# The max layers of a graph network: where the edge-attribute product is formed and where it is added to the gathered rows

## The chip, the core and the metric

The kernel runs on one core of a Trainium2 chip. The metric is the time of one execution in device microseconds. Three executions of the kernel before took 6829.79, 6830.46 and 6848.0 us, so the median is 6830.46 us. The kernel is one program: four graph layers with a feed-forward layer behind each, over 3125 nodes of 256 values and 50,000 edges that are sorted by their target node. Everything is float32 but a few masks. The change touches one function, `edge_max`, which runs twice in the fourth graph layer.

## The reference, cut to what matters

This is the fourth graph layer. `hv[src]` has 50,000 rows of 256 values, `he` is the edge attribute, 50,000 rows of 64 values.

```
hv = x @ W_in + b_in
for W, b in ((W_u0, b_u0), (W_u1, b_u1)):
    m = jnp.concatenate([hv[src], he], axis=-1)
    m = jax.nn.relu(m @ W + b)
    msg = jax.ops.segment_max(m, dst, num_segments=n)
    hv = jnp.where(has_in, msg + hv, hv)
return jax.nn.relu(hv @ W_ro + b_ro)
```

The product with `W` is split: the 256 upper rows of `W` are applied once per node (`hv @ W[0:256] + b`, stored in DRAM as `tab`), the 64 lower rows once per edge. So for each edge one row of `tab` is fetched, the product of the edge's 64 attributes with `W[256:320]` is added, and the running maximum over the edges of one target node is taken. The relu is the maximum with zero, which the scan starts from.

## The kernel before, in words

`edge_max` works on blocks of 512 edges (`GP`), 98 of them per call (`RG`), 196 in both calls. Names that the code uses: `P` is 128, `D` 256, `KD` 2 (halves of 128 of the 256 values), `Q` 4 (tiles of 128 edges in a block, and also the number of buffers in each ring), `W` 16, `EA` 64. Five engines run their own lists of instructions and meet at semaphores:

- POOL (L2452) gathers the 512 rows of `tab` into `max_rows`, with four indirect DMAs per block. The ring holds four blocks. Before it gathers block n it waits until block n-4 has been added up (semaphore `mixed`).
- SP (L2464, L2468) loads the attributes (`att`, already turned in DRAM: 64 partitions, edges along the free side) and the mask `same`, which is 0 where a new target node begins.
- TensorE, in `edges` (L2483), makes the attribute product: four products of 128 edges by 256 values into the banks `ps_e`, two signals `made` per block. In `turn` (L2493) it transposes the sum `msg` in eight pieces of 128 by 128 into `ps_t`, so that the 256 values stand on the partitions and the 512 edges along the free side; two signals `turned`. In `give_back` (L2504) it transposes the result of the scan back in eight pieces; two signals `returned`.
- VectorE, in `mix` (L2546), adds the gathered rows and `ps_e` into `msg`, two additions of 128x512 per block, and in `scan` (L2558) runs two scans of 128x512 per block, the running maximum, from `ps_t` into `run`.
- ScalarE (L2527) copies `ps_b` to `back` and writes 512 rows to DRAM (L2529).

The order on each engine is written out by hand. On TensorE one turn of the loop is `turn(n+1)`, `edges(n+2)`, `give_back(n)`; on VectorE `scan(n)`, `mix(n+2)`. TensorE's `turn(n)` waits for both additions of block n, its `edges(n)` for the additions of block n-1, since `ps_e` has one pair of banks; each addition waits for its `made`. PSUM's eight banks are used up: two for `ps_e`, four for `ps_t` (two blocks), two for `ps_b`.

Of the kernel before, what the change touches and what calls it, by code (L numbers as in the profile page):

```python
# [6 lines left out]
ALU = mybir.AluOpType  # L7
ACT = mybir.ActivationFunctionType
F32 = mybir.dt.float32
# [7 lines left out]
P = 128  # L17
# [2405 lines left out]
def edge_max(nc, g, table, w_dram):  # L2423


    with Phase(nc) as ph:
        sb, ps, sem = ph.sb, ph.ps, ph.sem
        rows = sb("max_rows", [P, W, D], F32)
        w = sb("w", [EA, D], F32)
        att = sb("att", [EA, W, P], F32)  # L2430
        same = sb("same", [P, Q, GP], BF16)
        msg = sb("msg", [P, W, D], F32)
        run = sb("run", [P, Q, KD, GP], F32)
        back = sb("back", [P, W, D], F32)
        ps_e = ps("ps_e", [P, 2, 512])
        ps_t = ps("ps_t", [P, 2, KD, 512])
        ps_b = ps("ps_b", [P, 2, 512])
# [3 lines left out]
        stored = [sem(f"stored{b}") for b in range(Q)]  # L2441
        w_in, zeroed, made, mixed, turned, ran, returned, taken = (sem(x) for x in (
            "w_in", "zeroed", "made", "mixed", "turned", "ran", "returned", "taken"))
        with nc.Block() as block:
            @block.gpsimd
            def _(pool):
                for n in range(RG):
                    b = n % Q
                    if n >= Q:
                        pool.wait_ge(mixed, 2 * (n - Q) + 2)  # L2450
                    for j in range(Q):
                        nc.gpsimd.indirect_dma_start(  # L2452
                            out=rows[:, b * Q + j, :], out_offset=None, in_=table,
                            in_offset=bass.IndirectOffsetOnAxis(ap=g.src_r[:, n * Q + j:n * Q + j + 1], axis=0)
                        ).then_inc(got[b], 16)

            @block.sync
            def _(sp):
                sp.dma_start(w[:], w_dram).then_inc(w_in, 16)
                for n in range(RG):  # L2460
                    b = n % Q
                    if n >= Q:
                        sp.wait_ge(made, 2 * (n - Q) + 2)
                    sp.dma_start(att[:, b * Q:(b + 1) * Q, :], g.ins["attr_t"][n * Q:(n + 1) * Q, :, :].rearrange("r e l -> e r l")  # L2464
                                 ).then_inc(att_in[b], 16)
                    if n >= Q:
                        sp.wait_ge(ran, 2 * (n - Q) + 2)
                    sp.dma_start(same[:, b, :], g.same_rows[n * GP:(n + 1) * GP].partition_broadcast(P)).then_inc(same_in[b], 16)  # L2468
# [3 lines left out]
            def _(pe):  # L2472
# [3 lines left out]
                def edges(n):  # L2476
                    b = n % Q
                    pe.wait_ge(att_in[b], 16 * (n // Q) + 16)
                    for k in range(2):
                        if n:  # L2480
                            pe.wait_ge(mixed, 2 * (n - 1) + k + 1)
                        for j in range(2):
                            ins = t.matmul(ps_e[:, k, j * D:(j + 1) * D], att[:, b * Q + 2 * k + j, :], w[:], start=True, stop=True)  # L2483
                        ins.then_inc(made, 1)

                def turn(n):
                    b = n % Q
                    if n >= 2:
                        pe.wait_ge(ran, 2 * (n - 2) + 2)
                    pe.wait_ge(mixed, 2 * n + 2)  # L2490
                    for c in range(KD):
                        for j in range(Q):
                            ins = t.transpose(ps_t[:, n % 2, c, j * P:(j + 1) * P], msg[:, b * Q + j, c * P:(c + 1) * P], g.ident[:])  # L2493
                        ins.then_inc(turned, 1)

                def give_back(n):
                    b = n % Q
                    pe.wait_ge(ran, 2 * n + 2)
                    for k in range(2):
# [35 lines left out]
            def _(dve):  # L2535
                v = nc.vector

                def mix(n):
                    b = n % Q
                    dve.wait_ge(got[b], 64 * (n // Q) + 64)  # L2540
                    if n >= Q:
                        dve.wait_ge(turned, KD * (n - Q) + KD)
                    for k in range(2):
                        dve.wait_ge(made, 2 * n + k + 1)
                        s = b * Q + 2 * k
                        v.tensor_tensor(msg[:, s:s + 2, :], rows[:, s:s + 2, :],  # L2546
                                        ps_e[:, k, :].rearrange("p (j d) -> p j d", j=2), ALU.add).then_inc(mixed, 1)

                def scan(n):
# [4 lines left out]
                    for c in range(KD):  # L2554
                        dve.wait_ge(turned, KD * n + c + 1)
                        if n:
                            dve.wait_ge(ran, KD * (n - 1) + c + 1)
                        v.tensor_tensor_scan(run[:, b, c, :], same[:, b, :], ps_t[:, n % 2, c, :], run[:, (b - 1) % Q, c, GP - 1:GP],  # L2558
                                             ALU.mult, ALU.max).then_inc(ran, 1)

                v.memset(run[:, Q - 1, :, :], 0.0).then_inc(zeroed, 1)
                dve.wait_ge(zeroed, 1)
                mix(0)
                mix(1)
                for n in range(RG):
                    scan(n)
                    if n + 2 < RG:
                        mix(n + 2)

# [503 lines left out]
```

## Time and profile before

| what | value |
|---|---|
| median of three executions | 6830.46 us |
| span of the profiled execution | 6822.1 us |
| first call of `edge_max` | about 5143 to 5795 us of the span |
| second call | about 5859 to 6511 us |
| TensorE busy in the span | 4796.2 us (70%) |
| VectorE busy | 3317.7 us (49%) |
| POOL busy | 3256.3 us (48%) |

The execution that was profiled took 6822.1 us from its first instruction to its last; the median of the timed ones is 8.4 us, 0.12%, above that. Times in the rows are microseconds from the start of the span. `PE` is TensorE's matmul side and `PEld` its weight loads, `DVE` is VectorE, `ACT` ScalarE, `SPq` and `ACTq` the issuing of DMAs. `PEclk` or the granted clock is the share of TensorE's full clock: 1.00 is 2.4 GHz, 0.50 is 1.2 GHz. What stands in brackets behind a row is how long the engine was idle before it and what ended that. A float32 matmul shows as two instructions in the trace, a transpose as one, so one block has eight `edges` instructions, eight of `turn` and eight of `give_back`. The names behind "DMA" in such brackets can be another transfer's that uses the same semaphore.

### The profile page before, as it was taken

To read this page: it belongs to the slowest core of one execution; us is meant where nothing else is said; L and a number is where in the kernel's file an instruction comes from. 1 tells how busy PE (TensorE), PEld (TensorE's weight loads), DVE (VectorE), ACT (ScalarE), POOL (GpSimd) and SP (SyncE) were. 2 spreads that over 40 slices of the span, in tenths; PEclk is the share of its full clock that TensorE was granted. 3 is DMA by queue.
4 is the path that set the end of the run, shared out by engine and by line. 5 is a ranking of instruction groups with operands and counts; after the bars stand their busy time and mean duration, and the time that the engine had idled before them with its cause. 6 is when DMAs were issued, how large, how long until landed. Compare 5 with 4: busy or idle time off the path is not lost. (4 is left out here: it accounts for less than half of the span.)

```text
span 6822.1 us, 83340 instructions
## 1 busy us (share of the span) xinstructions
PE 4796.2 (70%) x21859; PEld 3705.9 (54%) x21860; DVE 3317.7 (49%) x8140; ACT 1583.2 (23%) x4023; POOL 3256.3 (48%) x2940
## 2 busy tenths in 40 slices
PE   3666576999844438699959566466567877688868
PEld 2666455677433326477759434244445666566645
DVE  5544467323433337622331466588434555355554
ACT  1000075333100008300014222265221111111121
POOL 2666677777566648300020444564325555555510
PEclk8555588999866769899969655598677777777778
DMA  4888655000288856376646344486436776577710
GB/s 131 271 265 272 189 191 168 8 1 1 62 279 283 276 191 235 120 250 219 195 158 211 113 139 138 148 311 232 138 119 176 203 200 196 158 202 202 204 61 24
DMA packets 751400, 1183.52 MB, mean 173 GB/s; under 512 B 100921, under 2 KB 528682, under 8 KB 750982
## 3 DMA queue, kind: packets, MB, share of 16 engines
q1 hardware_dynamic: 366758, 553.94, 26.0%
q0 software_dynamic: 135904, 356.79, 18.8%
q10 hardware_dynamic: 248448, 269.39, 11.7%
q8 instruction: 125, 2.05, 0.1%
q14 instruction: 165, 1.35, 0.1%
HBM read 818.22 MB, written 361.10 MB: 173 GB/s over the span
## 5 line engine op out<-in xcount | busy, mean ns | idle before, releaser
L2452 POOL DMA_INDIRECT max_rows<-tab,src_r x784 | 743.0, 948 | 607.1 <-DVE msg L2546 292.0
L403 POOL DMA_INDIRECT counts<-put_n,put_at x400 | 565.6, 1414 | 212.6 <-issue 134.8
L1009 POOL DMA_INDIRECT late_rows<-tab,src_a x416 | 418.4, 1006 | 317.7 <-DMA slot_rows<-late_rows 177.5
L2546 DVE TENSOR_TENSOR msg<-max_rows,ps_e 128x512 f32<-128x512 f32 x392 | 265.8, 687 | 557.3 <-PE ps_e L2483 158.2
L986 PE MATMUL ps_b<-q,sel_t 128*128 x832 | 277.8, 499 | 367.1 <-DVE sel_t L905 251.4
L707 POOL DMA_INDIRECT logit_rows<-tab,src_a x416 | 416.9, 1002 | 247.9 <-DVE logits L927 136.0
L707 POOL DMA_INDIRECT logit_rows<-tab_kv,src_a x416 | 396.8, 954 | 284.7 <-issue 125.1
L2483 PE MATMUL ps_e<-w,att 64*128 64x256 f32 x1568 | 515.1, 482 | 24.6 <-DMA att<-in_attr_t 17.2
L2558 DVE TENSOR_TENSOR_SCAN run<-same,run,ps_t 128x512 f32<-128x512 bf16 x392 | 479.4, 1265 | 9.8 <-remote 5.5
L2527 ACT ACTIVATE back<-ps_b 128x512 f32<-128x512 f32 x392 | 222.4, 596 | 1094.4 <-PE ps_b L2504 463.3
L826 PE MATMUL ps_a<-msg,sel 128*128 128x264 f32 (+1 forms) x1664 | 412.8, 397 | 90.2 <-DVEq L758 46.7
L2493 PE MATMUL ps_t<-ident,msg 128*128 128x128 f32 x1568 | 299.2, 355 | 232.1 <-DVE msg L2546 227.1
L1520 PE MATMUL ps_a<-side,blocks 128*128 128x512 f32 x1950 | 460.3, 392 | 0.8 <-PE ps_a L1520 0.6
L1937 POOL DMA_INDIRECT slot_rows<-xn,into x100 | 101.9, 1019 | 745.0 <-DVE into L1929 716.1
L986 PEld LDWEIGHTS ps_b<-q,sel_t 128*128 128x128 f32 x832 | 203.7, 254 | 441.7 <-issue 404.0
L2483 PEld LDWEIGHTS ps_e<-w,att 64*128 64x128 f32 x1568 | 354.4, 238 | 135.0 <-issue 73.8
L986 PE MATMUL ps_b<-et,sel_t 128*128 x832 | 246.7, 370 | 252.8 <-DMA att<-in_attr_t 160.6
L826 PEld LDWEIGHTS ps_a<-msg,sel 128*128 128x128 f32 x1664 | 303.7, 191 | 199.0 <-DVE odd L772 58.2
L1520 PEld LDWEIGHTS ps_a<-side,blocks 128*128 128x128 f32 x1950 | 366.1, 188 | 83.0 <-issue 3.1
L638 PE MATMUL ps_o<-w,rows_t 128*128 128x256 f32 (+4 forms) x1000 | 322.9, 455 | 99.2 <-issue 70.0
L2493 PEld LDWEIGHTS ps_t<-ident,msg 128*128 128x128 f32 x1568 | 254.4, 189 | 251.3 <-issue 247.3
L915 DVE CUSTOM_DVE_ANT_0 prod<-logit_rows,ps_b 128x256 f32<-128x256 f32 x416 | 150.2, 417 | 421.9 <-DMA att<-in_attr_t 335.7
(482 smaller groups left out, 9786.7 us busy)
## 6 DMA issues: line engine op xcount, KB each, us to landing
blocks<-counts SPq DMA_DIRECT2D x390, 320.0 KB
slot_rows<-logit_rows ACTq DMA_DIRECT2D x208, 512.0 KB
edge_rows<-slot_rows SPq DMA_DIRECT2D x208, 512.0 KB
seg_rows<-back ACTq DMA_DIRECT2D x196, 512.0 KB
slot_rows<-late_rows SPq DMA_DIRECT2D x104, 512.0 KB
sum_rows<-slot_rows SPq DMA_DIRECT2D x104, 512.0 KB
counts<-zeros ACTq DMA_DIRECT2D x130, 320.0 KB
wf<-in_L_ffn_W SPq DMA_DIRECT2D x57, 512.0 KB
```

The source lines that it names most:

```text
L403: nc.gpsimd.indirect_dma_start(out=g.counts, out_offset=bass.IndirectOffsetOnAxis(ap=g.put_at[:, j:j + 1], axis=0), in_=g.put_n[:, j:j + 1 ...
L638: ins = nc.tensor.matmul(ps_o[:, (n % DEPTH) * NB + b, 0:c1 - c0], turned_rows(n, q), w[:, q // KD, q % KD, c0:c1], start=q == 0, stop=q = ...
L707: self.nc.gpsimd.indirect_dma_start(out=self.rows[:, (n % Q) * Q + j, :], out_offset=None, in_=table, in_offset=bass.IndirectOffsetOnAxis( ...
L826: nc.tensor.matmul(ps_a[:, n % 8, 0:C], sel[:, b % 2, j, :], rhs, start=True, stop=True).then_inc(summed, 1)
L986: ins = nc.tensor.matmul(product(b, j), sel_t[:, b % 2, j, :], node_cols[:, ds(tiles[j], 1), :].rearrange("p a c -> p (a c)"), start=True, ...
L1009: self.nc.gpsimd.indirect_dma_start(out=self.rows[:, b * Q + j, :], out_offset=None, in_=self.g.tab, in_offset=bass.IndirectOffsetOnAxis(a ...
L1520: ins = nc.tensor.matmul(ps_a[:, q % 2, :], blocks[:, k % RC, n % CH, :], both(side[:, n, :, :]), start=n == 0, stop=i == 0 and n == NT - 1)
L2452: nc.gpsimd.indirect_dma_start(out=rows[:, b * Q + j, :], out_offset=None, in_=table, in_offset=bass.IndirectOffsetOnAxis(ap=g.src_r[:, n ...
L2483: ins = t.matmul(ps_e[:, k, j * D:(j + 1) * D], att[:, b * Q + 2 * k + j, :], w[:], start=True, stop=True)
L2493: ins = t.transpose(ps_t[:, n % 2, c, j * P:(j + 1) * P], msg[:, b * Q + j, c * P:(c + 1) * P], g.ident[:])
L2546: v.tensor_tensor(msg[:, s:s + 2, :], rows[:, s:s + 2, :], ps_e[:, k, :].rearrange("p (j d) -> p j d", j=2), ALU.add).then_inc(mixed, 1)
L2558: v.tensor_tensor_scan(run[:, b, c, :], same[:, b, :], ps_t[:, n % 2, c, :], run[:, (b - 1) % Q, c, GP - 1:GP], ALU.mult, ALU.max).then_in ...
```

## The change

VectorE's addition is gone. TensorE forms the attribute product already turned, with the weights as the loaded side and the 512 edges as the moving side, straight into the banks that the scan reads (`start=True, stop=False`). The gathered rows are then transposed onto it, accumulating in PSUM (`start=False`, with `is_transpose`). `ps_e` and `msg` go away; the banks that become free give `ps_t` a third block (`R = 3`). POOL now waits for `turned` of block n-4 in place of `mixed`. `made` is signalled once per block and is waited for by SP alone. `edges(n)` waits for the scan of block n-3, half by half. `turn(n)` waits for the gathered rows themselves. VectorE runs only scans.

```
-        ps_e = ps("ps_e", [P, 2, 512])
-        ps_t = ps("ps_t", [P, 2, KD, 512])
+        ps_t = ps("ps_t", [P, R, KD, 512])
...
                     if n >= Q:
-                        pool.wait_ge(mixed, 2 * (n - Q) + 2)
+                        pool.wait_ge(turned, KD * (n - Q) + KD)
...
-                        sp.wait_ge(made, 2 * (n - Q) + 2)
+                        sp.wait_ge(made, n - Q + 1)
...
-                    for k in range(2):
-                        if n:
-                            pe.wait_ge(mixed, 2 * (n - 1) + k + 1)
-                        for j in range(2):
-                            ins = t.matmul(ps_e[:, k, j * D:(j + 1) * D], att[:, b * Q + 2 * k + j, :], w[:], start=True, stop=True)
-                        ins.then_inc(made, 1)
+                    for c in range(KD):
+                        if n >= R:
+                            pe.wait_ge(ran, KD * (n - R) + c + 1)
+                        ins = t.matmul(ps_t[:, n % R, c, :], w[:, c * P:(c + 1) * P], att[:, b, :], start=True, stop=False)
+                    ins.then_inc(made, 1)
 
                 def turn(n):
                     b = n % Q
-                    if n >= 2:
-                        pe.wait_ge(ran, 2 * (n - 2) + 2)
-                    pe.wait_ge(mixed, 2 * n + 2)
+                    pe.wait_ge(got[b], 64 * (n // Q) + 64)
                     for c in range(KD):
                         for j in range(Q):
-                            ins = t.transpose(ps_t[:, n % 2, c, j * P:(j + 1) * P], msg[:, b * Q + j, c * P:(c + 1) * P], g.ident[:])
+                            ins = t.matmul(ps_t[:, n % R, c, j * P:(j + 1) * P], rows[:, b * Q + j, c * P:(c + 1) * P], g.ident[:],
+                                           start=False, stop=j == Q - 1, is_transpose=True)
                         ins.then_inc(turned, 1)
...
-                def mix(n):
-                    b = n % Q
-                    dve.wait_ge(got[b], 64 * (n // Q) + 64)
-                    if n >= Q:
-                        dve.wait_ge(turned, KD * (n - Q) + KD)
-                    for k in range(2):
-                        dve.wait_ge(made, 2 * n + k + 1)
-                        s = b * Q + 2 * k
-                        v.tensor_tensor(msg[:, s:s + 2, :], rows[:, s:s + 2, :],
-                                        ps_e[:, k, :].rearrange("p (j d) -> p j d", j=2), ALU.add).then_inc(mixed, 1)
...
-                mix(0)
-                mix(1)
                 for n in range(RG):
                     scan(n)
-                    if n + 2 < RG:
-                        mix(n + 2)
```

On TensorE, the start of a call before the change, in the program's order (`ps_e<-w,att` is `edges`, `ps_t<-ident,msg` is `turn`, `ps_b<-ident,run` is `give_back`; the size is what one instruction of the program writes):

```order
L2483 MATMUL ps_e<-w,att 128x256 x8
L2493 MATMUL ps_t<-ident,msg 128x128 x16
L2483 MATMUL ps_e<-w,att 128x256 x4
L2504 MATMUL ps_b<-ident,run 128x128 x8
L2493 MATMUL ps_t<-ident,msg 128x128 x8
```

And the same place after it:

```order
L2481 MATMUL ps_t<-att,w 128x512 x4
L2489 MATMUL ps_t<-ident,max_rows 128x128 x16
L2481 MATMUL ps_t<-att,w 128x512 x2
L2501 MATMUL ps_b<-ident,run 128x128 x8
L2489 MATMUL ps_t<-ident,max_rows 128x128 x8
```

The order of the three steps is kept. A block has two products of 512 columns where it had four of 256, and the transposes read the gathered rows instead of the sum.

On VectorE the same place, as a piece of the difference (`msg<-max_rows,ps_e` is `mix`, the other is `scan`; the rows that alternate to the end of the call are cut):

```order
-L2561 MEMSET run 128x1024
-L2546 TENSOR_TENSOR msg<-max_rows,ps_e 128x512 x4
-L2558 SCALAR_TENSOR_TENSOR run<-same,run,ps_t 128x512 x2
-L2546 TENSOR_TENSOR msg<-max_rows,ps_e 128x512 x2
```

```order
L2547 MEMSET run 128x1024
L2544 SCALAR_TENSOR_TENSOR run<-same,run,ps_t 128x512 x196
```

Behind the change, the second of these, the 196 scans of a call stand in one row, with nothing between them.

## Rows read from the trace of the kernel before

**Rows 1.** Windows, both calls: busy us per engine, granted clock, DMA share, GB/s.

```profile
5143.00:5795.00 652.00, 514.94 (x2352) 407.04 (x2352) 365.41 (x393) 111.15 (x196) 371.48 (x392) 0.75 0.72 197
5859.00:6511.00 652.00, 521.19 (x2352) 412.85 (x2352) 365.55 (x393) 111.24 (x196) 371.51 (x392) 0.74 0.72 197
```

**Rows 2.** Groups by line in the first call: busy us, mean ns, idle before.

```profile
L2452 POOL DMA_INDIRECT max_rows<-tab,src_r x392 | 371.5, 948 | 319.9 <-DVE msg L2546 146.8 <-issue 113.2 <-POOLq L98 59.9
L2558 DVE TENSOR_TENSOR_SCAN run<-same,run,ps_t 128x512 f32<-128x512 bf16 x196 | 239.7, 1265 | 3.9 <-DMA moe_y<-y 3.5 <-issue 0.4
L2546 DVE TENSOR_TENSOR msg<-max_rows,ps_e 128x512 f32<-128x512 f32 x196 | 132.9, 687 | 279.4 <-DMA moe_y<-y 134.3 <-PE ps_e L2483 72.2 <-issue 61.1
```

**Rows 3.** Timeline of TensorE: start, us, engine, line, operation; at 1.2 GHz, then 2.4 GHz.

```profile
5230.24 1.91 PE L2493 MATMUL ps_t<-ident,msg 128*128 128x128 f32 x8
5232.08 3.77 PE L2483 MATMUL ps_e<-w,att 64*128 64x256 f32 x8
5235.79 1.97 PE L2504 MATMUL ps_b<-ident,run 128*128 128x128 f32 x8
5237.55 1.91 PE L2493 MATMUL ps_t<-ident,msg 128*128 128x128 f32 x8
...
5242.75 1.06 PE L2493 MATMUL ps_t<-ident,msg 128*128 128x128 f32 x8
5243.74 1.99 PE L2483 MATMUL ps_e<-w,att 64*128 64x256 f32 x8
5245.67 1.09 PE L2504 MATMUL ps_b<-ident,run 128*128 128x128 f32 x8
5246.61 1.06 PE L2493 MATMUL ps_t<-ident,msg 128*128 128x128 f32 x8
5247.60 1.99 PE L2483 MATMUL ps_e<-w,att 64*128 64x256 f32 x8
5249.52 1.17 PE L2504 MATMUL ps_b<-ident,run 128*128 128x128 f32 x8
```

**Rows 4.** Timeline of the other engines: one addition in rows 3, then just behind them.

```profile
5235.90 0.69 DVE L2546 TENSOR_TENSOR msg<-max_rows,ps_e 128x512 f32<-128x512 f32 x1 [0.92 <-PE ps_e L2483]
...
5251.64 0.95 POOL L2452 DMA_INDIRECT max_rows<-tab,src_r  x1 [0.30 <-issue]
5254.54 1.29 DVE L2546 TENSOR_TENSOR msg<-max_rows,ps_e 128x512 f32<-128x512 f32 x2 [5.72 <-DMA moe_y<-y]
5254.62 1.09 ACT L2527 ACTIVATE back<-ps_b 128x512 f32<-128x512 f32 x2 [4.64 <-DMA head_row<-in_L_gnn_att_dst]
5255.97 1.30 PE L2493 MATMUL ps_t<-ident,msg 128*128 128x128 f32 x5 [5.29 <-DVE msg L2546]
```

**Rows 5.** What TensorE's transposes waited for in both calls: us, times.

```profile
  DVE msg L2546: 227.1, 56
```

**Rows 6.** Windows of 3.4 us around rows 3 and 4, columns as in rows 1.

```profile
5237.40:5240.80 3.40, 3.40 (x14) 2.85 (x13) 1.54 (x2) 0.80 (x2) 2.48 (x4) 0.55 0.56 157
...
5251.00:5254.40 3.40, 0.00 (x0) 0.00 (x0) 0.00 (x0) 0.00 (x0) 1.28 (x2) 0.95 0.92 298
5254.40:5257.80 3.40, 1.83 (x8) 1.57 (x8) 3.26 (x4) 1.09 (x2) 1.40 (x2) 0.50 0.44 154
```

**Rows 7.** Timeline of TensorE in a later stage: float32 products of 512 columns.

```profile
6642.55 1.88 PE L2703 MATMUL ps_l<-wz,xt 128*128 128x512 f32 x4
6644.27 1.88 PE L2708 MATMUL ps_f<-wfx,xt 128*128 128x512 f32 x4
```

**Rows 8.** Windows there, columns as in rows 1.

```profile
6640.00:6660.00 20.00, 20.00 (x84) 11.67 (x83) 13.76 (x27) 6.41 (x12) 0.00 (x0) 1.00 0.00 0
```

**Rows 9.** All gathers of both calls: ns min/median/max, first and last start in us.

```profile
L2452 POOL DMA_INDIRECT max_rows<-tab,src_r x784: 943/949/959, 5143.3 to 6488.7; - x196
```

**Rows 10.** Timeline, start of the first call.

```profile
5147.05 0.95 POOL L2452 DMA_INDIRECT max_rows<-tab,src_r  x1 [0.31 <-issue]
5152.81 1.28 DVE L2546 TENSOR_TENSOR msg<-max_rows,ps_e 128x512 f32<-128x512 f32 x2 [8.98 <-DMA max_rows<-tab,src_r]
```

More of the change, by code:

```diff
@@ L2423, in edge_max @@
 def edge_max(nc, g, table, w_dram):
+    R = 3
     with Phase(nc) as ph:
@@ L2429, in edge_max @@
         w = sb("w", [EA, D], F32)
-        att = sb("att", [EA, W, P], F32)
+        att = sb("att", [EA, Q, GP], F32)
         same = sb("same", [P, Q, GP], BF16)
-        msg = sb("msg", [P, W, D], F32)
         run = sb("run", [P, Q, KD, GP], F32)
         back = sb("back", [P, W, D], F32)
-        ps_e = ps("ps_e", [P, 2, 512])
-        ps_t = ps("ps_t", [P, 2, KD, 512])
+        ps_t = ps("ps_t", [P, R, KD, 512])
         ps_b = ps("ps_b", [P, 2, 512])
@@ L2441, in edge_max @@
         stored = [sem(f"stored{b}") for b in range(Q)]
-        w_in, zeroed, made, mixed, turned, ran, returned, taken = (sem(x) for x in (
-            "w_in", "zeroed", "made", "mixed", "turned", "ran", "returned", "taken"))
+        w_in, zeroed, made, turned, ran, returned, taken = (sem(x) for x in (
+            "w_in", "zeroed", "made", "turned", "ran", "returned", "taken"))
         with nc.Block() as block:
@@ L2462, in _ @@
                     if n >= Q:
-                        sp.wait_ge(made, 2 * (n - Q) + 2)
-                    sp.dma_start(att[:, b * Q:(b + 1) * Q, :], g.ins["attr_t"][n * Q:(n + 1) * Q, :, :].rearrange("r e l -> e r l")
+                        sp.wait_ge(made, n - Q + 1)
+                    sp.dma_start(att[:, b, :].rearrange("e (r l) -> e r l", l=P), g.ins["attr_t"][n * Q:(n + 1) * Q, :, :].rearrange("r e l -> e r l")
                                  ).then_inc(att_in[b], 16)
                     if n >= Q:
-                        sp.wait_ge(ran, 2 * (n - Q) + 2)
+                        sp.wait_ge(ran, KD * (n - Q) + KD)
                     sp.dma_start(same[:, b, :], g.same_rows[n * GP:(n + 1) * GP].partition_broadcast(P)).then_inc(same_in[b], 16)
@@ L2497, in give_back @@
                     b = n % Q
-                    pe.wait_ge(ran, 2 * n + 2)
+                    pe.wait_ge(ran, KD * n + KD)
                     for k in range(2):
@@ L2557, in scan @@
                             dve.wait_ge(ran, KD * (n - 1) + c + 1)
-                        v.tensor_tensor_scan(run[:, b, c, :], same[:, b, :], ps_t[:, n % 2, c, :], run[:, (b - 1) % Q, c, GP - 1:GP],
+                        v.tensor_tensor_scan(run[:, b, c, :], same[:, b, :], ps_t[:, n % R, c, :], run[:, (b - 1) % Q, c, GP - 1:GP],
                                              ALU.mult, ALU.max).then_inc(ran, 1)
```

## The prediction

> **What bounds the kernel now.** I read the windows of the two calls first. Each takes 652 us for 98 blocks, 6.65 us a block and 1304 us in all, and no engine is full: TensorE is busy for 515 and 521 us, VectorE for 365, POOL for 371, and the clock granted to TensorE is 0.75 and 0.74, so it is at 1.2 GHz for half of the time [rows 1]. The groups by line show who waits for whom: POOL for VectorE's additions, these for TensorE and for something named a DMA [rows 2], TensorE's transposes for the additions again [rows 5]. It is a loop of engines, not one of them.
>
> The timeline says what one turn of the loop costs. At 1.2 GHz TensorE goes without a gap and a block takes 5237.55 - 5230.24 = 7.31 us; at 2.4 GHz it takes 5246.61 - 5242.75 = 3.86 us [rows 3]. POOL needs four gathers of 0.95 us with 0.30 us between them, 5.0 us a block [rows 4, 9]. So POOL alone would give 5.0, and 6.65 is a mixture of blocks at 7.31, blocks at 3.86, and stops.
>
> A stop is seen behind the fast blocks. TensorE's records end its products of a block at 5249.59 and its transposes back at 5250.69 [rows 3], yet the addition that needs nothing but these products, rows gathered long before, and an idle VectorE begins at 5254.54, and ScalarE's copy, which waits for transposes back alone, at 5254.62 [rows 4]. Two engines are set free within 0.1 us, 5 and 4 us after the work they waited for. I read this as TensorE's signals arriving late, in a stretch in which POOL issues gathers without a pause; they arrive 2 us after the last of these gathers ended at 5252.59 [rows 4]. At 1.2 GHz the signals are prompt: products that end at 5235.85 [rows 3] set free an addition at 5235.90 [rows 4]. The bracket's "DMA" I take to be the shared semaphore. The transposes then begin at 5255.97, after 5.29 us without work, and the clock falls: it is 0.95 in the window with no matmul and 0.50 in the next [rows 6]. Over both calls TensorE's transposes wait 56 times for the additions, 227.1 us, 4.06 us each [rows 5]. So the loop is: fast blocks, a stop, the clock down, slow blocks, the clock up again.
>
> **The change, part by part.** *The products.* Eight instructions of 256 columns a block become four of 512. At 2.4 GHz the eight take 5245.67 - 5243.74 = 1.93 us from their start to the next step's [rows 3], and four float32 ones of 512 columns take 6644.27 - 6642.55 = 1.72 us [rows 7] in a stretch at clock 1.00 [rows 8]. These load 128 rows where ours load 64; the row has no other difference. That is -0.21 us a block. At 1.2 GHz the eight take 5235.79 - 5232.08 = 3.71 us [rows 3]; twice 1.72 would be 3.44. No row shows 512 columns at 1.2 GHz, so between nothing and -0.27; I take -0.2 at either clock. 196 x 0.2 = 39 us, all on the path, since TensorE paces the blocks at either clock. Bounds 0 and -53.
>
> *The transposes.* Still eight of 128x128 a block, one instruction each. That they add to what stands in PSUM is shown by no row. Lower bound nothing; upper bound, if each were handled as an ordinary float32 product in two instructions, eight times 0.12 us more at 2.4 GHz (a transpose is (5243.74 - 5242.75) / 8 = 0.12 us, [rows 3]), about +1 us a block and 196 us. I take 0: same operation, same operand sizes.
>
> *The additions.* 392 of 0.687 us leave VectorE, twice 132.9, 266 us [rows 2]. Where TensorE runs without a gap that is worth nothing, since VectorE is idle for over 40% of a call [rows 1]. It counts where a stop ends: from the moment the late signal is seen to the first transpose is 5255.97 - 5254.54 = 1.43 us, two additions and a handover [rows 4]. After the change no transpose waits for VectorE or for a signal of TensorE's own, only for gathered rows, and those are there early: the fourth gather of the first block begins at 5147.05 and ends at 5148.00, and the addition starts 4.8 us later [rows 10]. 56 stops x 1.43 = 80 us.
>
> *What the late signals meet now.* `turned` sets the scan free, the scan `give_back`. Between the end of `turn(n)` and `give_back(n)` TensorE has `edges(n+1)`, `give_back(n-1)`, `turn(n+1)`, `edges(n+2)`: at 2.4 GHz 1.72 + 0.94 + 0.99 + 1.72 = 5.4 us [rows 3, 7], and two scans take 2.5 us [rows 2]. So a `turned` that is 2.9 us late costs nothing, where a late `made` cost at once. This could end the stops, or move them to `give_back`. There are also fewer signals, five a block for six, and 20 matmul instructions for 24. Against it stands the next part. I count both as 0 and keep the ends as rivals.
>
> *The moved waits.* POOL is let go by `turned(n-4)`, not by `mixed(n-4)`, so a row buffer is held until its transposes end, about 1 us longer in a stop and up to `give_back` and `turn` longer otherwise: 1.8 us at 2.4 GHz, 3.6 at 1.2 [rows 3]. Queued behind POOL's wait are only its own gathers. A block's gathers take 4.7 us and land within 4.8 [rows 9, 10], 9.5 us, and four fast blocks are 4 x 3.65 = 14.6 us; the ring is still deep enough. `edges(n)` waits for the scan of block n-3, which at 2.4 GHz is two blocks, 7.3 us, behind its `turned`: 0. SP's DMAs, their sizes and their order stay, and so does all that ScalarE and its queue do: 0.
>
> *The clock.* Shorter stops would leave it up more often; I put 0, since each stop left would still be 4.06 - 1.43 = 2.6 us.
>
> Sum: 6822.1 - 39 - 80 = 6703 us of span, and with the 8.4 us by which the median stands above the span, 6712 us. Range of this case alone, with the bounds of the products and half to twice the gain at the stops: 6620 to 6790 us.
>
> **The rivals.** *A, POOL sets the pace.* The stops and with them most of the slow blocks go. A call then is 392 gathers x 1.25 = 490 us and what follows the last gather, 6511 - 6488.7 = 22 us [rows 1, 9]: 512 for 652, 2 x 140 = 280 us less, 6550 us. For it: the slack of 2.9 us, two scans a block that need 2.5 of 5.0 us. Against it: signals came late exactly while POOL issued without a pause, and here it would never pause.
>
> *B, the stops stay as long.* They end when POOL pauses, not when VectorE is done, so taking out the additions only moves the wait to `give_back`. Then only the products count: 6830 - 39 = 6791 us. For it: DVE and ACT are set free together, 2 us after POOL's last gather [rows 4].
>
> *C, slower.* Now one late signal, `turned`, holds the scan and POOL too, and the message buffer that let the additions run ahead is gone. Each burst of late signals then empties the pipe, TensorE stands long enough for the clock to fall, and the blocks run at 1.2 GHz with 7.1 us each. All of them slow: 98 x 7.1 + 22 = 718 us a call, 2 x 66 = 132 us more, 6962 us; nine in ten slow and the rest at POOL's 5.0: 6.89 a block, 6877 us. It decides from the point where four in five blocks are slow (0.8 x 7.1 + 0.2 x 5.0 = 6.7). At present, 0.51 of 652 us over 7.31 is 45 of 98 [rows 1, 3]. A rule speaks for this rival. The trace first: the clock rises near the end of the window 5237.40 to 5240.80, whose mean is 0.55 [rows 6], since the blocks behind it have the short durations, and most of what TensorE did there and just before were sixteen transposes from 5235.79 to 5239.46 [rows 3]. The Trainium skill, TensorE: Matmul & The Clock Gate, Part 4: PE-mode transpose, says that transposes do not count as work for the clock in the way matmuls do, and that it does not rise for them; by that rule a kernel with fewer ordinary matmul instructions would stay low and give C's 6962 us. The trace contradicts it here, so I leave C small.
>
> *D, the accumulating transposes cost more than plain ones.* By the bound above up to +196 us; with half of it and the gains 6810 us.
>
> **How the numbers follow.** Likeliest case 0.47, A 0.20, B 0.14, C 0.13, D 0.06. The range for 8 in 10 goes from A's 6550 less a little, 6540, to 6845, which leaves out C and a small part of A and D. A measurement of this kernel can tell 0.3%, 20 us, from no change. Faster than 6810: the likeliest case, A, nearly all of B, some of D, 0.81. Within 20 us: 0.06. Slower: C and the bad half of D, 0.13.
>
> **What would show it.** In the changed profile: no row of `msg`; 784 instructions of 512 columns where 1568 of 256 stood, 1.7 us a block at 2.4 GHz; transposes as long as before (0.12 us each at 2.4 GHz); the idle time before them near nothing and waits of TensorE before `give_back` in its place; a call of about 590 us and a granted clock of 0.75 to 0.8. A call near 512 us with POOL busy in 73% of it shows A; one of 630 us with 56 stops of 4 us shows B; a clock below 0.6 shows C. I am wrong if the stops were not set by late signals, or if they grow as much as the additions gave.

## The result

The changed kernel takes 6725.02 us (median of 4 runs, 6715.43 to 6727.1), the kernel before 6831.03 us beside it. The ratio is 0.9836, with a 95% interval of 0.9821 to 0.9851: 1.6% faster, a small gain that is clear of the noise. The forecast was 6712 us. The profiled execution spans 6721.4 us where the one of before spans 6822.1, 100.7 us less.

The first view is the windows of the two calls, which answer to [rows 1]; the columns are the same (length; busy us of TensorE, its weight loads, VectorE, ScalarE, POOL; granted clock; DMA share; GB/s):

```profile
5143.00:5743.00 600.00, 450.89 (x1960) 283.03 (x1960) 242.98 (x197) 112.39 (x196) 370.45 (x392) 0.80 0.76 214
5807.00:6412.00 605.00, 454.29 (x1960) 284.34 (x1960) 242.26 (x197) 112.21 (x196) 370.49 (x392) 0.80 0.75 213
```

The windows of the calls are 52 and 47 us shorter, 99 of the 100.7 us. TensorE was busy for 514.94 + 521.19 = 1036.1 us [rows 1] and is now for 905.2: 131 us less. VectorE lost its additions and is busy for 122 and 123 us less. POOL's gathers cost what they cost, 370.5 us a call. The clock is 0.80 where it was 0.75 and 0.74.

The groups by line in both calls come next (count; busy us, mean ns; idle time of the engine just before them and what ended it). Of before these are the four that the comparison needs and that no row ahead of the prediction gives for both calls:

```profile
L2452 POOL DMA_INDIRECT max_rows<-tab,src_r x784 | 743.0, 948 | 607.1 <-DVE msg L2546 292.0 <-issue 226.4 <-POOLq L98 88.8
L2483 PE MATMUL ps_e<-w,att 64*128 64x256 f32 x1568 | 515.1, 482 | 24.6 <-DMA att<-in_attr_t 17.2 <-issue 3.7 <-DVE msg L2546 3.6
L2493 PE MATMUL ps_t<-ident,msg 128*128 128x128 f32 x1568 | 299.2, 355 | 232.1 <-DVE msg L2546 227.1 <-issue 4.9
L2504 PE MATMUL ps_b<-ident,run 128*128 128x128 f32 x1568 | 271.4, 327 | 18.2 <-issue 11.7 <-DVE run L2558 4.9 <-ACT back L2527 1.6
```

And of the changed kernel:

```profile
L2451 POOL DMA_INDIRECT max_rows<-tab,src_r x784 | 740.9, 945 | 510.7 <-issue 213.4 <-POOLq L98 90.1 <-PE ps_t L2489 82.8
L2544 DVE TENSOR_TENSOR_SCAN run<-same,run,ps_t 128x512 f32<-128x512 bf16 x392 | 483.4, 1269 | 710.2 <-PE ps_t L2489 188.6 <-PE ps_b L2501 165.3 <-DMA moe_y<-y 154.8
L2481 PE MATMUL ps_t<-att,w 64*128 64x512 f32 x784 | 445.7, 694 | 17.8 <-DMA att<-in_attr_t 17.8
L2501 PE MATMUL ps_b<-ident,run 128*128 128x128 f32 x1568 | 267.1, 319 | 283.6 <-ACT back L2524 219.5 <-issue 52.9 <-DVE run L2544 10.9
L2489 PE MATMUL ps_t<-ident,max_rows 128*128 128x128 f32 x1568 | 249.0, 312 | 1.9 <-DMA max_rows<-tab,src_r 1.8
```

Three things are to be seen. TensorE no longer waits before its transposes (1.9 us for 232.1) but before it gives back (283.6 us for 18.2). Its idle time as a whole did not fall: 24.6 + 232.1 + 18.2 = 274.9 us before, 303.3 now. And POOL is idle for 96 us less (510.7 for 607.1). So TensorE gained no time from shorter waits; it gained it from instructions that ran at 2.4 GHz instead of 1.2. Of 196 groups of eight transposes (two calls of 98 blocks), 80 had the short duration before (under 1.15 us from the first start to the last end) and 138 have it now.

The timeline of TensorE around one stop (start, us, engine, line, operation; in the bracket the idle time before it) answers to [rows 3]:

```profile
5292.17 1.04 PE L2489 MATMUL ps_t<-ident,max_rows 128*128 128x128 f32 x8
5293.13 1.98 PE L2481 MATMUL ps_t<-att,w 64*128 64x512 f32 x4
5295.05 1.09 PE L2501 MATMUL ps_b<-ident,run 128*128 128x128 f32 x8
5295.97 1.04 PE L2489 MATMUL ps_t<-ident,max_rows 128*128 128x128 f32 x8
...
5308.86 1.09 PE L2501 MATMUL ps_b<-ident,run 128*128 128x128 f32 x8
5309.79 1.04 PE L2489 MATMUL ps_t<-ident,max_rows 128*128 128x128 f32 x8
5310.76 1.98 PE L2481 MATMUL ps_t<-att,w 64*128 64x512 f32 x4
5321.71 1.94 PE L2501 MATMUL ps_b<-ident,run 128*128 128x128 f32 x8 [8.98 <-ACT back L2524]
5323.45 1.92 PE L2489 MATMUL ps_t<-ident,max_rows 128*128 128x128 f32 x8
```

A block at 2.4 GHz takes 5295.97 - 5292.17 = 3.80 us (3.86 in [rows 3]). Then TensorE stands for 8.98 us. What it waits for is seen on the other engines, which answers to [rows 4]:

```profile
5317.70 0.95 POOL L2451 DMA_INDIRECT max_rows<-tab,src_r  x1 [0.30 <-issue]
5320.97 1.26 ACT L2524 ACTIVATE back<-ps_b 128x512 f32<-128x512 f32 x2 [13.28 <-DMA tab<-hw]
5321.86 2.45 DVE L2544 TENSOR_TENSOR_SCAN run<-same,run,ps_t 128x512 f32<-128x512 bf16 x2 [8.38 <-DMA moe_y<-y]
5321.99 0.94 POOL L2451 DMA_INDIRECT max_rows<-tab,src_r  x1 [3.34 <-DMA moe_y<-y]
```

What ScalarE copies at 5320.97 are the transposes of 5308.86, which ended at 5309.95, 11 us earlier. VectorE and POOL, which wait for other signals of TensorE, are set free within 1.1 us of it, all of them 2.3 us or more after POOL's last gather ended at 5318.65. That is the pattern of [rows 4], with another engine at the end of the wait. The windows there (columns as in [rows 1]) show what it does to the clock:

```profile
5312.80:5316.20 3.40, 0.00 (x0) 0.00 (x0) 0.68 (x1) 0.00 (x0) 2.74 (x3) 1.00 0.91 229
5316.20:5319.60 3.40, 0.00 (x0) 0.00 (x0) 0.00 (x0) 0.00 (x0) 1.89 (x2) 0.50 0.54 160
5319.60:5323.00 3.40, 1.29 (x6) 1.32 (x7) 1.14 (x1) 1.30 (x3) 0.94 (x1) 0.50 0.07 25
```

### The profile page after: what moved, and what is told of

Read it like the earlier page. It is cut to its first block and busy times, and to the rows that moved or that the text cites. A ratio compares the mean times of both kernels' runs of the same rounds, so it can differ in the third digit from the quotient of the medians.

```text
span 6721.4 us, 80988 instructions
## 1 busy us (share of the span) xinstructions
PE 4661.4 (69%) x21075; PEld 3448.9 (51%) x21076; DVE 3071.9 (46%) x7748; ACT 1586.1 (24%) x4023; POOL 3241.1 (48%) x2940
## 3 DMA queue, kind: packets, MB, share of 16 engines
q8 instruction: 118, 1.93, 0.1%
## 5 line engine op out<-in xcount | busy, mean ns | idle before, releaser
L2451 POOL DMA_INDIRECT max_rows<-tab,src_r x784 | 740.9, 945 | 510.7 <-issue 213.4
L1009 POOL DMA_INDIRECT late_rows<-tab,src_a x416 | 416.6, 1001 | 323.7 <-DMA slot_rows<-late_rows 178.2
L2501 PE MATMUL ps_b<-ident,run 128*128 128x128 f32 x1568 | 267.1, 319 | 283.6 <-ACT back L2524 219.5
L2524 ACT ACTIVATE back<-ps_b 128x512 f32<-128x512 f32 x392 | 224.6, 596 | 989.7 <-DMA tab<-hw 281.0
L2481 PE MATMUL ps_t<-att,w 64*128 64x512 f32 x784 | 445.7, 694 | 17.8 <-DMA att<-in_attr_t 17.8
L2501 PEld LDWEIGHTS ps_b<-ident,run 128*128 128x128 f32 x1568 | 201.9, 162 | 460.6 <-issue 369.7
L986 PEld LDWEIGHTS ps_b<-et,sel_t 128*128 128x128 f32 x832 | 207.7, 310 | 269.9 <-issue 262.0
```

Of the source, the lines that this page charges most:

```text
L986: ins = nc.tensor.matmul(product(b, j), sel_t[:, b % 2, j, :], node_cols[:, ds(tiles[j], 1), :].rearrange("p a c -> p (a c)"), start=True, ...
L1009: self.nc.gpsimd.indirect_dma_start(out=self.rows[:, b * Q + j, :], out_offset=None, in_=self.g.tab, in_offset=bass.IndirectOffsetOnAxis(a ...
L2451: nc.gpsimd.indirect_dma_start(out=rows[:, b * Q + j, :], out_offset=None, in_=table, in_offset=bass.IndirectOffsetOnAxis(ap=g.src_r[:, n ...
L2481: ins = t.matmul(ps_t[:, n % R, c, :], w[:, c * P:(c + 1) * P], att[:, b, :], start=True, stop=False)
L2501: ins = t.transpose(ps_b[:, k, j * D + c * P:j * D + (c + 1) * P], run[:, b, c, (2 * k + j) * P:(2 * k + j + 1) * P], g.ident[:])
L2524: nc.scalar.activation(back[:, s:s + 2, :].rearrange("p j d -> p (j d)"), ps_b[:, k, :], ACT.Copy).then_inc(taken, 1)
```

## The experiments

Twelve kernels were run. All ratios are to the kernel before on the same chip. The runs were spread over several chips, on which the kernel before took 6783 to 6846 us (6831 beside the changed one), so microseconds of different rows compare to about 1%. "Call" is the first call, from the start of TensorE's first record to the start of its last; "idle" is TensorE's idle time before its three groups of matmuls in both calls together.

| kernel | ratio (95%) | call, us | idle, us |
|---|---|---|---|
| before | 1 | 646.3 | 274.9 |
| changed | 0.9836 (0.9821 to 0.9851) | 592.8 | 303.3 |
| e1 plain loads, POOL silent | 0.922 (0.9189 to 0.925) | 380.4 | 20.3 |
| e2 as e1, POOL gathers narrow rows | 0.9821 (0.9791 to 0.9851) | 588.1 | 259.6 |
| e8 kernel before, POOL silent | 0.9251 (0.923 to 0.9272) | 385.7 | 21.8 |
| e3 products of 256 columns | 0.984 (0.9816 to 0.9865) | 588.1 | 236.7 |
| e4 POOL a block less ahead | 0.9826 (0.9803 to 0.9849) | 582.9 | 216.7 |
| e5 two `ps_t` pairs | 0.9838 (0.9819 to 0.9857) | 588.8 | 271.5 |
| e6 three signals for five | 0.985 (0.9832 to 0.9869) | 595.5 | 285.0 |
| e7 additions, nobody waits | 0.983 (0.9812 to 0.9848) | 585.9 | 273.3 |
| e9 crossing, short work | 0.984 (0.9823 to 0.9856) | 590.0 | 220.8 |
| e12 crossing, additions' work | 0.9844 (0.9828 to 0.986) | 592.4 | 218.6 |
| e10 two `ps_b` pairs | 0.9833 (0.9817 to 0.9849) | 590.5 | 204.9 |
| e11 and `give_back` later | 0.9832 (0.9815 to 0.985) | 591.4 | 215.2 |

### Is it POOL that delays the signals?

**e1**, in the changed kernel, takes the gathers out and loads plain rows with one transfer of SyncE a block:

```diff
-                    for j in range(Q):
-                        nc.gpsimd.indirect_dma_start(out=rows[:, b * Q + j, :], ...).then_inc(got[b], 16)
+                    pass
...
+                        sp.wait_ge(turned, KD * (n - Q) + KD)
+                    first = n % 6 * GP
+                    sp.dma_start(rows[:, b * Q:(b + 1) * Q, :], table[first:first + GP, :].rearrange("(j p) d -> p j d", p=P)).then_inc(got[b], 16)
```

> The changed kernel, but the 512 rows of a block are fetched by one plain load from SP's queue (consecutive rows of the table, so the gather is left out and the output is not the reference's); POOL is silent in both calls, the bytes moved are the same. Theory 1, TensorE's signals are held back while POOL issues gathers: no stops, clock near 1.0, TensorE sets the pace with 3.8 us a block, a call 375 to 420 us for 595, the kernel about 6340 us. Rival, the data traffic holds them back (DMA share 0.76 in a call): the stops stay or get denser, a call 550 us or more, since the traffic per us would rise.

**e2** is e1 with POOL issuing as many gathers as before, of 16 values a row, into a buffer that nothing reads:

```diff
+                            out=narrow[:, b * Q + j, :], out_offset=None, in_=table.rearrange("n (k s) -> (n k) s", s=16),
...
+                        ).then_inc(fetched[b], 16)
```

> As the run with plain loads, and beside them POOL issues the same 392 gathers per call into a small side tile, 16 values a row in place of 256: the same number of rows and the same issuing, a sixteenth of the bytes. (Output not the reference's.) Theory 1, it is POOL's issuing: the stops of 2 to 14 us in front of the transposes back return, a call 570 to 620 us. Rival, the traffic: a call as with plain loads, or POOL's own 490 us.

Measured: 6260.65 us for e1, 6669.01 for e2. The transposes back in e1, then in e2 (groups by line, as above), and the first call of e1 (window):

```profile
L2499 PE MATMUL ps_b<-ident,run 128*128 128x128 f32 x1568 | 213.9, 279 | 2.8 <-DVE run L2542 2.8
```

```profile
L2510 PE MATMUL ps_b<-ident,run 128*128 128x128 f32 x1568 | 273.2, 325 | 242.6 <-ACT back L2533 175.9 <-issue 48.5 <-DVE run L2553 17.7
```

```profile
5108.70:5489.10 380.40, 378.78 (x1960) 237.59 (x1960) 240.06 (x196) 105.39 (x195) 0.00 (x0) 0.98 1.05 336
```

With POOL silent there is no stop, the clock is 0.98, and a block takes 3.88 us. With POOL issuing gathers that TensorE does not wait for, a sixteenth as wide, the stops and the 588 us are back. It is the gathers, then, and neither their bytes nor the wait for the rows. POOL's issuing and the many small transfers that each gather starts (one for each row) were not taken apart; "POOL's issuing" below means both.

**e8** is the same edit as e1 in the kernel before, with SyncE's load waiting for `mixed`.

> The kernel before, with the gather of both calls left out: SyncE loads plain rows of the table, one transfer a block, and POOL is silent. The changed kernel with the same edit took 6261 us, 0.922 of the kernel before. Theory 1: the change's gain is that fewer signals cross between engines while POOL holds them up; with POOL silent the two kernels are the same within 15 us: 6250 to 6280 us, no stops, clock about 0.8. Theory 2: the additions cost time by themselves (VectorE's hop of 1.4 us in each block): 6320 to 6370 us, with TensorE idle ahead of its transposes as in the kernel before.

Measured: 6279.3 us. VectorE's two groups:

```profile
L2556 DVE TENSOR_TENSOR_SCAN run<-same,run,ps_t 128x512 f32<-128x512 bf16 x392 | 479.1, 1264 | 0.9 <-PE ps_t L2491 0.9
L2544 DVE TENSOR_TENSOR msg<-max_rows,ps_e 128x512 f32<-128x512 f32 x392 | 269.0, 687 | 42.3 <-PE ps_e L2481 13.2 <-DMA max_rows<-tab 4.5 <-issue 2.4
```

With POOL silent the two kernels are 18.6 us apart, on two chips, two runs each (0.9251 and 0.922, intervals that overlap), with the gathers 106. That is a little more than the 15 us of theory 1, and the time is inside its range: most of the gain exists only while POOL issues. The few microseconds left would be VectorE, which here is busy for 366 of 386 us a call and is idle for 0.9 us before its scans; the changed kernel's is busy for 240.

### Which part of the change gives the gain?

Each of the next runs puts one part back into the changed kernel. **e3**, the products in pieces of 256 columns:

```diff
-                        ins = t.matmul(ps_t[:, n % R, c, :], w[:, c * P:(c + 1) * P], att[:, b, :], start=True, stop=False)
+                        for h in range(2):
+                            ins = t.matmul(ps_t[:, n % R, c, h * D:(h + 1) * D], w[:, c * P:(c + 1) * P], att[:, b, h * D:(h + 1) * D], start=h == 0, stop=False)
```

> The changed kernel with each product of 512 columns cut into two of 256, so 4 products (8 instructions) a block as before the change, nothing else. By the prediction's term for the products it costs 0.2 us a block, 39 us: about 6764 us. If the clock went up in the changed kernel because fewer matmul instructions mean fewer held signals, more: up to 6790. If TensorE's shape costs nothing: 6725.

**e5**, the third pair of banks away: `R = 3` becomes `R = 2`.

> The changed kernel with two pairs of ps_t banks in place of three, so that the products of a block wait for the scan of two blocks before. Theory 1: TensorE's semaphore signals arrive late while POOL issues gathers, and it was the additions on VectorE, with their two hops in each block (made to the addition, mixed to the transposes), that made TensorE stop often and fall to the low clock; the third bank is beside the point, since the scan of block n-2 is long done. Then the ratio to the kernel before stays 0.980 to 0.988, and stops stay ahead of give_back (about 280 us). Theory 2: the gain is the third bank, which takes the scan's slowness off the path. Then the ratio is 0.995 to 1.005, and the products stop for ran.

**e7**, VectorE's additions back in number and size, behind each scan, on a buffer of their own:

```diff
+                        for k in range(2):
...
+                            v.tensor_tensor(spare[:, k, :, :], spare[:, k, :, :], spare[:, k, :, :], ALU.add).then_inc(cleared, 1)
```

> The changed kernel with two additions of 128x512 in each block put back on VectorE behind the scan, as in the kernel before, but on a buffer of their own in SBUF: nothing but VectorE's order waits for them. Theory 1: what cost time was that TensorE waited for the additions, not the time that they took on VectorE: ratio to the kernel before 0.980 to 0.988. Theory 2: what cost time was that the scan began later behind the additions: ratio 0.990 to 1.003, and scan's rows show more time between turned and its start.

**e9**, the crossing to VectorE back, with hardly any work in it:

```diff
-                    pe.wait_ge(got[b], 64 * (n // Q) + 64)
+                    pe.wait_ge(mixed, 2 * n + 2)
...
+                    dve.wait_ge(got[b], 64 * (n // Q) + 64)
+                    dve.wait_ge(made, n + 1)
+                    for k in range(2):
...
+                        v.memset(spare[:, k, :], 0.0).then_inc(mixed, 1)
```

> The changed kernel with the crossing to VectorE put back without its work: VectorE waits for the gather and for made as the additions did, at their place behind the scan, does two memsets of 128x16, each with a signal, and TensorE's transposes wait for these and no more for the gather itself. The memsets feed nothing. Theory 1: the chain TensorE to VectorE to TensorE in each block is what cost time, since made and turned reach VectorE late while POOL issues: TensorE stops ahead of its transposes again, and the ratio to the kernel before is 0.993 to 1.003. Theory 2: it needs the additions' own 1.3 us in that chain; with short ones most of the gain stays: 0.982 to 0.990.

**e12**, the same with the additions' work:

```diff
-                        v.memset(spare[:, k, :], 0.0).then_inc(mixed, 1)
+                        v.tensor_tensor(spare[:, k, :, :], rows[:, s:s + 2, :], rows[:, s:s + 2, :], ALU.add).then_inc(mixed, 1)
```

> As e9, but what VectorE does between the gather and the transposes is as long as the additions of the kernel before: two additions of 128x512 a block (of the gathered rows, into a buffer that nothing reads), for which the transposes wait. Left as in the changed kernel: three ps_t banks, POOL's wait on turned, products that wait only for the scan. The crossing with short work cost nothing (0.984), and the additions with nobody waiting cost nothing (0.983). Theory 1: the change gained because a stop no longer has the additions at its end, about 1.4 us between the late signal and the first transpose, and because the shorter stops leave the clock up for longer: here the stops are back as they were, ratio 0.995 to 1.005, and clock near 0.75. Theory 2: the gain came from what is left as in the changed kernel, above all POOL's wait, which lets it issue in fewer, longer stretches: ratio 0.980 to 0.988, clock near 0.775.

Measured: 0.984, 0.9838, 0.983, 0.984 and 0.9844. Every interval holds the changed kernel's 0.9836, and none reaches 0.99. None of these parts is the gain by itself: not the shape of the products, not the third bank, not VectorE's time, not the crossing, and not the crossing with all its work. In e12 the wait did go back to its old place, which is why this run counts most against my reasons (TensorE's transposes, both calls):

```profile
L2490 PE MATMUL ps_t<-ident,max_rows 128*128 128x128 f32 x1568 | 271.1, 329 | 173.5 <-DVE spare L2556 115.9 <-issue 57.6
```

The stops stand before the transposes again, 51 of over 1 us, but they are 2.5 us long (128.2 us in all) where those of before were 3.9 (59, 232.0 us).

### Do the stops go away with slack or with fewer signals?

**e4** lets POOL run three blocks ahead, not four:

```diff
-                    if n >= Q:
-                        pool.wait_ge(turned, KD * (n - Q) + KD)
+                    if n >= 3:
+                        pool.wait_ge(turned, KD * (n - 3) + KD)
```

> The changed kernel, but POOL waits for the transposes of block n-3 in place of n-4, so its unbroken runs of gathers end a block earlier. Theory 1 (a stop lasts until POOL pauses): stops become shorter, the long ones of 8 to 9 us go to about 4, and there are more of them; the kernel within 6700 to 6740 us. Rival, the depth of the ring is what hides the gathers' way from issue to landing (9.5 us): slower, a call over 620 us, the kernel over 6770.

**e6** signals `turned` and `returned` once a block:

```diff
-                        ins.then_inc(turned, 1)
+                    ins.then_inc(turned, 1)
...
-                        ins.then_inc(returned, 1)
+                    ins.then_inc(returned, 1)
```

> The changed kernel with turned and returned signalled once in a block (3 signals of TensorE in a block for 5); the scan and ACT start up to half a group of transposes (0.5 us at the full clock) later. Theory 1: while POOL issues, TensorE's signals are delivered one by one, 0.7 to 2.1 us apart, so 5 in a block of 3.8 us are more than get through, and 3 are not: the stops ahead of give_back shrink from about 280 us in the two calls to under 150, and the ratio to the kernel before falls to 0.960 to 0.975. Theory 2: signals wait for POOL's pauses whatever their number, so fewer do not help: ratio 0.980 to 0.988, or up to 0.995 from the later starts.

**e10** has two pairs of `ps_b` and two of `ps_t`; **e11** also issues each `give_back` a block later:

```diff
-                        if n:
-                            pe.wait_ge(taken, 2 * (n - 1) + k + 1)
+                        if n >= 2:
+                            pe.wait_ge(taken, 2 * (n - 2) + k + 1)
...
-                    give_back(n)
+                    if n:
+                        give_back(n - 1)
```

> The changed kernel with two pairs of ps_t banks (worth nothing by themselves: 0.9838 for 0.9836) and two pairs of ps_b banks, so that give_back waits for ACT's copies of two blocks before, not one. Theory 1: the stops ahead of give_back are late returned signals, of 2 to 9 us; one block more of slack (3.8 us) takes the short ones and shortens the long: give_back's idle time falls from about 280 to 100 to 160 us, ratio 0.965 to 0.978. Theory 2: POOL holds all of TensorE's signals until it pauses, and it pauses only when TensorE's turned reaches it, so more slack only moves the stop to the next wait (the products' on ran, the transposes' on the gather): ratio 0.980 to 0.988, same idle time in another row.

> As e10, and each give_back one block later in TensorE's order, so that its wait for the scan has a block more too. Theory 1 (slack helps): TensorE's idle time falls below e10's, ratio 0.955 to 0.975. Theory 2 (the stop moves): the idle time stands ahead of the products (ran) and of the transposes (gather), ratio 0.980 to 0.990.

Measured: 0.9826, 0.985, 0.9833 and 0.9832. Fewer signals do not help (e6 stands for 285 us), so theory 1 of e6 is refuted. e4 has the shorter stops that its theory 1 asked for (58 of over 1 us before the two groups of transposes, 3.0 us each, where the changed kernel has 54 of 4.8). A shorter ring and more slack do lower the idle time, to 217, 205 and 215 us from 303, but not the time of a call. In e10 the wait has moved to the products and the transposes, as theory 2 said, but it is a third shorter, which theory 2 did not say:

```profile
L2481 PE MATMUL ps_t<-att,w 64*128 64x512 f32 x784 | 506.8, 771 | 117.8 <-DVE run L2544 69.7 <-issue 30.0 <-DMA att<-in_attr_t 17.8
L2489 PE MATMUL ps_t<-ident,max_rows 128*128 128x128 f32 x1568 | 282.6, 322 | 84.3 <-issue 82.9 <-DMA max_rows<-tab,src_r 1.1
L2501 PE MATMUL ps_b<-ident,run 128*128 128x128 f32 x1568 | 271.6, 328 | 2.8 <-DVE run L2544 2.8
```

and what the stops lost, the clock took: products of 771 ns in the mean for 694, and 92 groups of transposes at the short duration for 138. That is seen throughout the table: eleven kernels (the changed one, e2 to e7, e9 to e12), POOL issuing in each, idle times from 205 to 303 us, and first calls from 583 to 596. No version beats the changed kernel by more than the measurement can tell.

## Why the prediction held, and where it did not

The time (6725 us measured, 6712 forecast) and most of what was to show it came out: no row of `msg`, 784 products, idle time before the transposes near nothing with waits before `give_back` in its place, calls of 593 and 598 us in TensorE's records (about 590 was said), a clock of 0.80. But one of the two signs of being wrong that the prediction names came out too: the stops grew although the additions were gone, from 3.9 us in the mean before the transposes to 4.9 before `give_back`, and TensorE's idle time rose where it should have fallen by 80 us. That the time was right is luck: the two terms that made up the sum, 39 and 80 us, were each worth nothing that the runs could tell, and the gain came through the clock, which stood in it at 0. By its steps:

*The products, -39 us: mis-sized, by all of it.* The four of 512 columns take 5295.05 - 5293.13 = 1.92 us from their start to the next step's; the eight of 256 took 1.93 [rows 3]. At 1.2 GHz the four take 3.71 us (5385.10 to 5388.81 in the changed kernel), as the eight did [rows 3]. The 1.72 us of [rows 7], which the prediction took for ours because "the row has no other difference" than the loaded rows, does not carry over, and the single records show why. Inside a group the instructions of 512 columns begin 0.43 us apart, whether they load 64 rows (changed kernel) or 128 ([rows 7]): the product itself costs the same. The 0.2 us lie at the two ends of our group: its first step takes 0.53 us and its last 0.52, and at both ends the weight load of the group that follows begins only 2 or 3 ns before the instruction that uses it. In the stretch of [rows 7] each load begins 2 ns behind the start of the product before, also where transposes follow, and no time is lost. So cutting the products differently could gain nothing: both cuts have the same two ends. What is special about these ends is that 64 loaded rows meet 128; no run varies that alone. e3 agrees with the whole term (0.984 for 0.9836), though it is weak evidence, since its idle time differs too (237 us). The lower bound of nothing was the value.

```profile
5385.10 3.78 PE L2481 MATMUL ps_t<-att,w 64*128 64x512 f32 x4
5388.81 1.97 PE L2501 MATMUL ps_b<-ident,run 128*128 128x128 f32 x8
```

*The transposes, 0: right.* Eight of them with accumulation take 1.04 us where plain ones took 1.06 [rows 3]. With that rival D is gone.

*The additions, -80 us: the step that failed.* It was "56 stops x 1.43 = 80 us", time from the late signal to the first transpose. TensorE's idle time rose by 28 us. And e12 put two additions of that length back between the signal and the transposes and lost nothing (0.9844). In this kernel a microsecond taken out of a stop is not a microsecond of the call, for the stops and the clock trade with each other.

*The late signals, 0:* the slack of 2.9 us did not end the stops. They moved to `give_back`, 53 of over 1 us with 4.9 us in the mean; that "could move them to `give_back`" was the right half of the sentence.

*The clock, 0: wrong, and it is where TensorE's gain is entered.* TensorE is busy for 131 us less, in fewer blocks at 1.2 GHz, and idle for 28 us more; with rounding at the edges of the windows that is the 99 us of both calls. The products gave nothing and a group of transposes 0.02 us, so all but a few of the 131 us are the clock's.

*The moved waits, 0: this is what the experiments leave.* I charged POOL's wait, from `mixed` to `turned`, as a loss that the ring would hide. That POOL was idle for 96 us less says nothing by itself, for the idle time of every engine with unchanged work shrinks with the call; ScalarE's did by 105 (1094.4 to 989.7). What did change is how POOL issues. In the first call's records POOL issued its 392 gathers in 76 stretches before (59 of them of four gathers, a pause at nearly each block) and in 42 now (mostly 8 or 12 gathers; a pause of over 0.6 us parts two stretches). All variants of the changed kernel with the gathers on have 53 or fewer. But this is as much effect as cause, and e7 with 27 stretches and gathers of 1043 ns takes as long as the changed kernel with 42.

So what is shown: the gain needs POOL's issuing (1.6% with it, 0.3% without, e1 against e8), and it is none of five parts of the change put back alone. What stays open: POOL's wait for `mixed`, the message buffer that makes this wait possible, and the sixth signal of a block (`made` twice) were never put back; a combination may be needed too. The products' wait for the additions was not put back either, but it can be struck from the list: `edges(n+2)` stands right behind `turn(n+1)`, which has waited for the same additions already, and only 3.6 us of the idle time before the products are put down to it in the rows of before. The kernel before with POOL waiting for `turned` would be the next run; it was not tried. Open too is what holds a call at 583 to 596 us in all of these kernels.

The rivals: *A*, POOL paces, needed the stops to go; POOL is busy in 62% of a call, and its own 1.25 us a gather give 490 of 593 us. *B* had the mechanism of the stops right, they only move to `give_back` and do not get shorter, but the products it counted on are worth nothing; by its price the time would be 6830. That the gain came all the same, through the clock, was in no case of mine. *C*, slower with the clock down, is refuted: 0.80 for 0.75. (Its two figures do not go together: the 6962 us include the 22 us behind the last gather, the 6877 do not; with them it would be about 6921.) The kernel now has 1960 TensorE instructions a call for 2352 and as many transposes as before, and the clock is higher. The rule of the Trainium skill, TensorE: Matmul & The Clock Gate, Part 4: PE-mode transpose, that the clock does not engage for transposes, would have let it fall. The trace contradicts it: in the changed kernel TensorE does nothing but sixteen transposes behind a stop, and the clock goes up within the second eight of them (windows from 5286.0 to 5288.9 us and on, columns as in [rows 1]):

```profile
5286.09 1.94 PE L2501 MATMUL ps_b<-ident,run 128*128 128x128 f32 x8 [8.98 <-ACT back L2524]
5287.82 1.57 PE L2489 MATMUL ps_t<-ident,max_rows 128*128 128x128 f32 x8
5289.33 1.98 PE L2481 MATMUL ps_t<-att,w 64*128 64x512 f32 x4
...
5286.00:5288.90 2.90, 2.81 (x14) 2.84 (x15) 2.45 (x2) 1.79 (x3) 1.90 (x3) 0.50 0.46 129
5288.90:5292.00 3.10, 3.10 (x15) 1.69 (x15) 2.45 (x2) 0.01 (x1) 2.49 (x3) 1.00 0.91 243
```

## What to carry to other kernels

When an engine's stops are followed by a lower clock, do not price a stop by its length: e10 took 98 us of idle time out of the changed kernel and gained nothing. Before pricing any edit in such a loop, silence the suspected disturber once (e1); it showed that 6% lay in POOL's issuing and not in the work that was being moved. And a duration for a group of products is taken from rows with the same kind of work before and behind it, for part of it lies at its ends.

## What the runs showed of the hardware

TensorE's signals reach other engines late while POOL issues indirect gathers without a pause and TensorE is at 2.4 GHz. It can be counted on ScalarE, which waits for transposes back alone, at those of its 392 copies before which it stood idle. In the changed kernel, where POOL had gathered for over 60% of the 2.5 us before, 55 of 108 copies at 2.4 GHz began over 1 us behind the end of the transposes, the latest 18.5 us, and 1 of 40 at 1.2 GHz; the other 39 began about 0.1 us behind it or sooner. In e1, with POOL silent and TensorE at 2.4 GHz, all 196 did. The slow clock is no guard against it, though: in e3 27 of 63 such copies at 1.2 GHz were over 1 us late. In the changed kernel's semaphore records of the stop above, `turned`, `made` and `returned` counts rose at 5307.07, 5308.51, 5312.18, 5316.43 and 5320.89 us, one at a time, and then four times within 0.2 us (5321.61 to 5321.79), after POOL's last gather ended at 5318.65; TensorE's last matmul had ended at 5312.74. Why POOL delays them no run tells.

Two additions with both operands in SBUF slow POOL's gathers (e7, both calls):

```profile
L2452 POOL DMA_INDIRECT max_rows<-tab,src_r x784 | 818.0, 1043 | 422.5 <-issue 218.3 <-POOLq L98 86.4 <-DMA moe_y<-y 45.5
```

1043 ns for 945; in the kernel before, where one operand of each addition was in PSUM, a gather took 948. In e12, whose additions also have both operands in SBUF, it took 1001 ns. The Trainium skill, GPSIMD Engine Reference, 1. Specifications, says that POOL shares its way into SBUF with VectorE and is held up by VectorE's instructions with two SBUF inputs. The trace agrees.
